# One scan over two channel groups instead of two scans in a selective-state-space kernel

## The chip, the cores and the metric

The program runs on 1 core of one Trainium2 chip, in one launch. The metric is the device time in microseconds (us). Before the change it was 1109.41 us, the median of three runs (1102.5 to 1112.57). The engines are named TensorE (PE in the rows, its weight loads PEld), VectorE (DVE), ScalarE (ACT), GpSimd (POOL) and SyncE (SP, which only issues transfers).

## The reference, cut to what matters

```python
xn = layernorm(x)                                    # (2, 1024, 512)
proj = xn @ W_in.T; x, gate = split(proj)            # 1024 channels each
x = silu(causal_conv4(x)); ssm = x @ W_x.T           # step sizes, B, C (16 states)
dt = softplus(rms(ts) @ W_dt.T + b_dt); A = -exp(A_log)
# scan over the 1024 tokens of a row, for each channel d and state n
state = state * exp(dt_t * A) + (dt_t * u_t) * B_t
y_t   = sum_n state * C_t
y = (y + x * D) * silu(gate);  s = y @ W_out.T
g = silu(top-2-of-8 mixture of experts(xn));         out = x + s * g
```

All is float32. The recurrence has 2 batch rows x 1024 channels x 16 states, 1024 tokens long. The rest (projections, the mixture of experts with its gather of rows, the output) is woven between the pieces of the recurrence.

## The kernel before, in words

**Tiling.** The 2048 tokens are cut into four chunks of `TC` = 512. Chunks 0 and 2 start a batch row ("even"), chunks 1 and 3 continue it ("odd"). A chunk has 8 tiles of 128 channels, so there are 32 tiles, numbered n. A tile has 128 x 16 recurrences; they are laid out over the 128 partitions in 16 units of 128 recurrences x 512 tokens. Four units are a quad (number m, four to a tile, 128 in all): its decays lie in the four banks of `sc` in PSUM (one bank holds 512 float32), its drives in one of four slots of `drive` in SBUF. Half a quad, two units side by side, is called a **pair** here: the low one (h = 0) and the high one (h = 1). There are 256 pairs.

**What a pair goes through.** GpSimd writes `drive` = dt*u*B for a quad (`drives`, L541), two quads or more ahead. ScalarE writes exp(dt*A) for the two units of a pair into `sc` (`decays`, L762), one ACTIVATE a unit. VectorE runs one scan a unit (`scans`, L1133) and multiplies both units by C (`products`, L1143). For 76 of the 128 low pairs GpSimd does that product instead (`low_products`, L554), and the scans of those write `drive`. TensorE sums the units of a channel (`sums`, L1391).

**What orders it.** Each engine has one queue, written out by hand tile by tile, and semaphores between the queues. `sc` has one copy: ScalarE may write the decays of a pair of quad m only when VectorE is done with the same pair of quad m - 1 (`low_ok`, `high_ok`, or `scan_ok` where GpSimd has the product). In even chunks ScalarE first copies the last column of both units to `state` (`keep_states`, L741) and waits for that copy; in odd chunks nothing is kept, and each scan starts from a column of `state`. ScalarE takes the pairs in the same order as VectorE, and between them its queue holds the softplus (L707 to L716), copies for the experts (L774, L785) and for the output (L798), the scaling of gathered rows (L831), and once a tile a block that no decay can pass: a table load, the silu of the gate, a table load (L906, L822, L914), just ahead of the decays of the high pair of the tile's third quad. That spot is called the **table place** here. In a unit's first scan VectorE waits only for the decay of that unit.

Of the kernel before, what the change touches and what calls it, by code (L numbers as in the profile page):

```python
# [7 lines left out]
ALU = mybir.AluOpType  # L8
ACT = mybir.ActivationFunctionType
# [8 lines left out]
PER_ROW = SEQ // TC  # L18
NT = D_IN // P
# [3 lines left out]
NQ = N // NG  # L23
CH = P // NG
NR = P // CH
# [7 lines left out]
RING = 4  # L33
# [39 lines left out]
def on_pool(m):  # L73
    return m % NQ in POOL_QUADS.get(m // NQ, ())


def dve_pairs(m):
    return m - pool_pairs(m)


def kept_states(m):
    c, rest = divmod(m, NQ * NT)
    kept = 2 * NQ * NT * ((c + 1) // 2)
    return kept + (2 * rest if c % PER_ROW < PER_ROW - 1 else 0)


def scan_moe(nc, x, wx_in, wg_in, wdt_in, wxp, wring, gate_w, means, a_log, conv_w, conv_b, d_skip,
             token_ids, route_consts, bc_dram, rep_rows, xn_rows, xnT_rows, order, slot_rows, s_rows, out):
    with ExitStack() as ctx:
        def sb(name, *shape, dtype=F32):  # L90
            return ctx.enter_context(nc.sbuf_tensor(name, [P, *shape], dtype))

        def ps(name, *shape):
            return ctx.enter_context(nc.psum_tensor(name, [P, *shape], F32))

        def sem(name):
            return ctx.enter_context(nc.semaphore(name))
# [3 lines left out]
        drive = sb("drive", RING, NR, TC)  # L101
        rep = sb("rep", 2, NR, 2, TC)
# [11 lines left out]
        x_pad = sb("x_pad", TC + K - 1)  # L114
        halo = sb("halo", NT, K - 1)
        no_halo = sb("no_halo", K - 1)
        t_e, t_w, t_l, t_r = sb("t_e", TC), sb("t_w", TC), sb("t_l", TC), sb("t_r", TC)
        dtu = sb("dtu", 2, TC)
        dt, u = dtu[:, 0, :], dtu[:, 1, :]
# [5 lines left out]
        state = sb("state", NT * UNITS)  # L125
        a_neg = sb("a_neg", NT * UNITS)
# [38 lines left out]
        sc = ps("sc_ps", NR, TC)  # L165
# [5 lines left out]
        first, second = x_ps[:, P:2 * P], x_ps[:, 2 * P:3 * P]  # L171
# [81 lines left out]
        abs_ok, exp_ok, ln_ok = sem("abs_ok"), sem("exp_ok"), sem("ln_ok")  # L253
        relu_ok, w_ok, log_mm = sem("relu_ok"), sem("w_ok"), sem("log_mm")
        sp_ok, dt_ok, dt_cp = sem("sp_ok"), sem("dt_ok"), sem("dt_cp")
        decay_ok, drive_ok, scan_ok = sem("decay_ok"), sem("drive_ok"), sem("scan_ok")
        state_ok = sem("state_ok")
        low_ok, high_ok, pool_ok = sem("low_ok"), sem("high_ok"), sem("pool_ok")
        sum_ok = sem("sum_ok")
        gated = sem("gated")  # L260
# [10 lines left out]
        def column(t, q, r):  # L271
            return t * UNITS + q * NR + r
# [7 lines left out]
        def drives_done(eng, count):  # L280
            eng.wait_ge(drive_ok, count)
# [193 lines left out]
        def _(pool):  # L475
# [68 lines left out]
            def low_products(m):  # L544
                n, q = divmod(m, NQ)
                if not on_pool(m):
                    return
                c, t = divmod(n, NT)
                pool.wait_ge(scan_ok, NR * m + 2)
                if c % PER_ROW < PER_ROW - 1:  # L550
                    pool.wait_ge(state_ok, kept_states(m) + 1)
                if t == 0:
                    pool.wait_ge(s_c[q], 16 * (c + 1))
                pool.tensor_tensor(drive[:, m % RING, 0:2, :], drive[:, m % RING, 0:2, :],  # L554
                                   c_all[:, q:q + 1, :].broadcast_to([P, 2, TC]), ALU.mult).then_inc(pool_ok, 1)
# [86 lines left out]
        def _(act):  # L642
# [88 lines left out]
            def keep_states(m, h):  # L731
                n, q = divmod(m, NQ)
                c, t = divmod(n, NT)
                if c % PER_ROW == PER_ROW - 1:
                    return
                lo = column(t, q, 2 * h)
                if h == 0 and on_pool(m):
                    last = drive[:, m % RING, 0:2, TC - 1]
                else:
                    last = sc[:, 2 * h:2 * h + 2, TC - 1]  # L740
                act.activation(state[:, lo:lo + 2], last, ACT.Copy).then_inc(state_ok, 1)  # L741

            def decays(m, h):
                n, q = divmod(m, NQ)
                if n >= TILES:
                    return
                t = n % NT
                if m:
                    if h:
                        act.wait_ge(high_ok, m)  # L750
                    elif on_pool(m - 1):
                        act.wait_ge(scan_ok, NR * (m - 1) + 2)
                    else:
                        act.wait_ge(low_ok, dve_pairs(m))
                    keep_states(m - 1, h)
                    if (m - 1) // (NQ * NT) % PER_ROW < PER_ROW - 1:
                        act.wait_ge(state_ok, kept_states(m - 1) + h + 1)
                if q == 0:
                    act.wait_ge(s_rep[n % 2][h], REP // 2 * (n // 2 + 1))
                for r in (2 * h, 2 * h + 1):  # L760
                    lo = column(t, q, r)
                    act.activation(sc[:, r, :], rep[:, n % 2, r, 0, :], ACT.Exp,  # L762
                                   scale=a_neg[:, lo:lo + 1]).then_inc(decay_ok, 1)

            def copy_slot_T(b, j):
                if j is None:
# [97 lines left out]
            act.copy(logit_T[:, :], f_ps[:, :]).then_inc(lgT_ok, 1)  # L864
            act.wait_ge(a_ok, 1)
            decays(0, 0)
            decays(0, 1)
            act.wait_ge(lg_d, 1)
            act.activation(weight, weight, ACT.Exp).then_inc(lg_e, 1)

            for n in range(TILES):
                c, t = divmod(n, NT)
                m = NQ * n
# [6 lines left out]
                if n:  # L880
                    decays(m, 1)
# [60 lines left out]
        def _(dve):  # L942
# [178 lines left out]
            def scans(m, h):  # L1121
                n, q = divmod(m, NQ)
                c, t = divmod(n, NT)
                if h == 0:
                    drives_done(dve, m + 1)
                follows = c % PER_ROW > 0
                if follows:
                    dve.wait_ge(state_ok, kept_states(m - NQ * NT) + h + 1)
                for r in (2 * h, 2 * h + 1):
                    lo = column(t, q, r)  # L1130
                    to = drive[:, m % RING, r, :] if h == 0 and on_pool(m) else sc[:, r, :]
                    dve.wait_ge(decay_ok, NR * m + r + 1)
                    dve.tensor_tensor_scan(to, sc[:, r, :], drive[:, m % RING, r, :],  # L1133
                                           state[:, lo:lo + 1] if follows else 0.0,
                                           ALU.mult, ALU.add).then_inc(scan_ok, 1)

            def products(m, h):
                n, q = divmod(m, NQ)
# [8 lines left out]
            def low(m):  # L1147
                scans(m, 0)
                if not on_pool(m):
                    products(m, 0)  # L1150

            def high(m):
                scans(m, 1)
                products(m, 1)
# [43 lines left out]
            for h in range(2):  # L1198
                scans(0, h)
                products(0, h)  # L1200
            route_weights()
            for n in range(TILES):
                c, t = divmod(n, NT)
                m = NQ * n
# [377 lines left out]
```

## Time and profile before

| | |
|---|---|
| median of three runs | 1109.41 us |
| profiled execution, own time | 1104.65 us |
| its span, first to last instruction | 1102.8 us |
| VectorE busy | 1025.4 us (93%) |
| GpSimd busy | 903.0 us (82%) |
| TensorE busy | 868.6 us (79%) |
| ScalarE busy | 730.2 us (66%) |

The profiled execution is one execution; what lies around its span is 1.85 us. The busy share is of the whole span; the first 84 us hold no scan of the recurrence. A row of the timeline with x2 is two instructions back to back, and its duration runs from the start of the first to the end of the second.

### The profile page before, as it was taken

What the parts mean: (1) busy time and instruction counts of PE and PEld (TensorE: products, weight loads), DVE (VectorE), ACT (ScalarE), POOL (GpSimd) and SP (SyncE); (2) the same over time, 40 slices, a digit from 0 to 9 for tenths busy, and PEclk for the clock granted to TensorE, in tenths of its full rate; (3) what the DMA queues carried; (4) which work ended last, traced back from release to release, by engine and by line L of the source; (5) the groups of instructions that cost most, each with busy time, mean ns of one, the idle gap of its engine ahead of it and who ended that gap; (6) DMA issues with size and microseconds to landing.
All of it is one profiled execution on the core that took longest, in us unless ns stands there. A gap on an engine that the chain in (4) does not pass through costs nothing.

```text
span 1102.8 us, 10141 instructions
## 1 busy us (share of the span) xinstructions
PE 868.6 (79%) x2722; PEld 317.1 (29%) x2722; DVE 1025.4 (93%) x1052; ACT 730.2 (66%) x1284; POOL 903.0 (82%) x353
## 2 busy tenths in 40 slices
PE   6954386899969998888854768989788998778577
PEld 3330122333323332333211222323223333223122
DVE  6759998999999999999999989999999989999997
ACT  2664666778766766777665766878767666666565
POOL 0019998998879899989889969798978978998895
PEclk9986678999989999999966979999998999799789
DMA  9345376656576566676743453865547656565714
GB/s 328 116 158 198 105 221 216 223 200 234 185 256 252 194 223 230 174 194 180 236 162 126 144 191 126 313 235 191 198 170 263 214 196 234 208 220 181 269 37 152
DMA packets 78089, 219.26 MB, mean 199 GB/s; under 512 B 15824, under 2 KB 17232, under 8 KB 71376
## 3 DMA queue, kind: packets, MB, share of 16 engines
q1 hardware_dynamic: 58096, 166.67, 44.4%
q10 hardware_dynamic: 12672, 31.46, 7.4%
q0 software_dynamic: 7264, 20.47, 6.7%
q8 instruction: 23, 0.38, 0.1%
q14 instruction: 34, 0.28, 0.1%
HBM read 176.85 MB, written 41.72 MB: 198 GB/s over the span
## 4 chain that ended last, share of the span: by engine, by line
DVE 34%; PE 24%; POOL 16%; issue 11%; ACT 7%; DMA 7%; SPq 1%; DVEq 0%; ACTq 0%; POOLq 0%
DVE sc_ps L1133 17%; POOL drive L541 10%; PE x_ps L1423 5%; DVE drive L1133 5%; PE f_ps L1376 4%; DVE drive L1143 3%; PE x_ps L1286 3%; POOL drive L554 3%; DMA rep<-rep_rows 3%; PE dt_ps L1351 3%; DMA x_slot<-xn_rows,slot_tok 3%; PE y_ps L1391 2%; DVE x_ps L1074 2%; PE sc_ps L1286 2%; ACT sc_ps L762 1%
## 5 line engine op out<-in xcount | busy, mean ns | idle before, releaser
L541 POOL TENSOR_TENSOR drive<-rep,b_all 128x2048 f32<-128x2048 f32 x128 | 580.3, 4538 | 118.1 <-DVEq L1017 77.4
L762 ACT ACTIVATE sc_ps<-rep,a_neg 128x512 f32<-128x512 f32 x512 | 332.0, 681 | 89.4 <-DVE drive L1143 63.1
L1133 DVE TENSOR_TENSOR_SCAN sc_ps<-sc_ps,state,drive 128x512 f32<-128x512 f32 x180 | 220.8, 1273 | 6.9 <-ACT sc_ps L762 6.9
L1143 DVE TENSOR_TENSOR drive<-sc_ps,c_all 128x1024 f32<-128x1024 f32 x180 | 220.4, 1224 | 6.2
L1391 PE MATMUL y_ps<-drive,stack 128*32 128x512 f32 x1024 | 156.7, 690 | 87.9 <-DVE drive L1143 60.4
L1133 DVE TENSOR_TENSOR_SCAN sc_ps<-sc_ps,drive 128x512 f32<-128x512 f32 x180 | 210.0, 1212 | 3.2 <-ACT sc_ps L762 2.3
L554 POOL TENSOR_TENSOR drive<-drive,c_all 128x1024 f32<-128x1024 f32 x76 | 179.3, 2359 | 23.3 <-ACT state L741 22.6
L1376 PE MATMUL f_ps<-w_ring,xT_slot 128*128 128x512 f32 x368 | 174.5, 619 | 14.4 <-ACT xT_slot L774 14.4
L1351 PE MATMUL dt_ps<-xnT,w_g 128*128 128x512 f32 x232 | 118.7, 659 | 21.3 <-ACT dtu L729 20.1
L1376 PEld LDWEIGHTS f_ps<-w_ring,xT_slot 128*128 128x128 f32 x368 | 70.5, 199 | 118.6 <-issue 118.3
L1133 DVE TENSOR_TENSOR_SCAN drive<-sc_ps,state,drive 128x512 f32<-128x512 f32 x76 | 93.1, 1266 | 2.8 <-ACT sc_ps L762 2.8
L1133 DVE TENSOR_TENSOR_SCAN drive<-sc_ps,drive 128x512 f32<-128x512 f32 x76 | 88.4, 1203 | 0.0
L1286 PE MATMUL x_ps<-xnT,w_x 128*128 128x512 f32 x192 | 88.2, 602 | 0.0
L1423 PE MATMUL x_ps<-w_out,xy 128*128 128x512 f32 x176 | 84.9, 629 | 0.0
L1391 PEld LDWEIGHTS y_ps<-drive,stack 128*32 128x32 f32 x1024 | 22.1, 114 | 185.5 <-issue 144.1
L1351 PEld LDWEIGHTS dt_ps<-xnT,w_g 128*128 128x128 f32 x232 | 46.5, 211 | 97.1 <-issue 97.1
L741 ACT ACTIVATE state<-sc_ps 128x2 f32<-128x2 f32 x90 | 15.1, 168 | 82.6 <-DVE drive L1143 80.5
L508 POOL DMA_INDIRECT x_slot<-xn_rows,slot_tok x46 | 45.5, 990 | 21.6 <-PE f_ps L1365 15.7
L1385 PE MATMUL y_ps<-xy,diag 128*128 128x512 f32 x64 | 37.5, 670 | 28.0 <-DVE xy L1160 28.0
L1365 PE MATMUL f_ps<-ident,x_slot 128*128 128x128 f32 x184 | 29.7, 286 | 33.3 <-DMA x_slot<-xn_rows,slot_tok 29.8
L1327 PE MATMUL dt_ps<-dt_in,w_dt 128*128 128x512 f32 x64 | 43.1, 762 | 15.2 <-DVE dt_in L1190 14.5
L1286 PEld LDWEIGHTS x_ps<-xnT,w_x 128*128 128x128 f32 x192 | 35.0, 190 | 52.4 <-issue 52.2
(184 smaller groups left out, 1057.7 us busy)
## 6 DMA issues: line engine op xcount, KB each, us to landing
rep<-rep_rows SPq DMA_DIRECT2D x128, 512.0 KB
w_ring<-wring SPq DMA_DIRECT2D x46, 1024.0 KB
rep_rows<-dtu ACTq DMA_DIRECT2D x32, 512.0 KB, 3.2
slot_rows<-y_slot ACTq DMA_DIRECT2D x46, 256.0 KB, 4.4
w_g<-wg_in SPq DMA_DIRECT2D x32, 256.0 KB
w_x<-wx_in SPq DMA_DIRECT2D x24, 256.0 KB
xn_rows<-rep SPq DMA_DIRECT2D x16, 256.0 KB, 2.5
b_all<-bc_rows SPq DMA_DIRECT2D x16, 256.0 KB, 4.4
```

Of the source, the lines that this page charges most:

```text
L508: pool.indirect_dma_start(x_slot[:, :], None, xn_rows[:, :], bass.IndirectOffsetOnAxis(ap=slot_tok[:, m:m + 1], axis=0)).then_inc(s_gx, 16)
L541: pool.tensor_tensor(drive[:, m % RING, :, :], rep[:, n % 2, :, 1, :], b_all[:, q:q + 1, :].broadcast_to([P, NR, TC]), ALU.mult).then_inc( ...
L554: pool.tensor_tensor(drive[:, m % RING, 0:2, :], drive[:, m % RING, 0:2, :], c_all[:, q:q + 1, :].broadcast_to([P, 2, TC]), ALU.mult).then ...
L762: act.activation(sc[:, r, :], rep[:, n % 2, r, 0, :], ACT.Exp, scale=a_neg[:, lo:lo + 1]).then_inc(decay_ok, 1)
L1133: dve.tensor_tensor_scan(to, sc[:, r, :], drive[:, m % RING, r, :], state[:, lo:lo + 1] if follows else 0.0, ALU.mult, ALU.add).then_inc(s ...
L1143: dve.tensor_tensor(drive[:, m % RING, 2 * h:2 * h + 2, :], sc[:, 2 * h:2 * h + 2, :], c_all[:, q:q + 1, :].broadcast_to([P, 2, TC]), ALU. ...
L1286: last = pe.matmul(x_bank(j), w(h), xnT[:, c % 2, h, :], start=(h == 0), stop=(h == HK - 1))
L1327: pe.matmul(dt_ps[:, :], w_dt[:, t, :], dt_in[:, :], start=True, stop=True).then_inc(dt_mm, 1)
L1351: mm = pe.matmul(gate_bank(c, t)[:, :], w_g[:, h, :], xnT[:, c % 2, h, :], start=(h == 0), stop=(h == HK - 1))
L1376: last = pe.matmul(f_ps[:, :], xT_slot[:, h, :], w_ring[:, j % 2, h, :], start=(h == 0), stop=(h == HK - 1))
L1391: last = pe.matmul(y_ps[CH * r:CH * (r + 1), :], stack[:, :], drive[:, m % RING, r, :], start=False, stop=(m % NQ == NQ - 1))
L1423: last = pe.matmul(bank, xy[:, c % 2, t, P * i:P * (i + 1)], w_out[:, t, :], start=(t == 0), stop=(t == NT - 1))
```

## The change

A pair's two scans become one over 1024 columns. Between the two units stands a decay of zero: ScalarE writes 0 to column 0 of the second unit's decays (a copy of one column from `no_halo`) and the exponentials to the other 511. With a decay of zero the second unit starts from its own first drive. In even chunks that is all. In odd chunks the second unit has a state to start from: ScalarE computes the exponential of the second unit's first column apart (`step1`) and, behind the two decays, adds `step1` * `state` to the first column of the second unit's drive, in place, after waiting for `step1_ok` and for GpSimd's drive. VectorE waits for the zero, for both decays and, in odd chunks, for that addition.

```diff
+def followers(m):
+    c, rest = divmod(m, NQ * NT)
+    return 2 * NQ * NT * (c // PER_ROW) + (2 * rest if c % PER_ROW else 0)
...
+        step1 = sb("step1", 2)
...
-                for r in (2 * h, 2 * h + 1):
-                    lo = column(t, q, r)
-                    act.activation(sc[:, r, :], rep[:, n % 2, r, 0, :], ACT.Exp,
-                                   scale=a_neg[:, lo:lo + 1]).then_inc(decay_ok, 1)
+                lo, odd = column(t, q, 2 * h), 2 * h + 1
+                act.activation(sc[:, odd, 0:1], no_halo[:, 0:1], ACT.Copy).then_inc(cut_ok, 1)
+                follows = n // NT % PER_ROW > 0
+                if follows:
+                    act.activation(step1[:, h:h + 1], rep[:, n % 2, odd, 0, 0:1], ACT.Exp,
+                                   scale=a_neg[:, lo + 1:lo + 2]).then_inc(step1_ok, 1)
+                act.activation(sc[:, 2 * h, :], rep[:, n % 2, 2 * h, 0, :], ACT.Exp,
+                               scale=a_neg[:, lo:lo + 1]).then_inc(decay_ok, 1)
+                act.activation(sc[:, odd, 1:], rep[:, n % 2, odd, 0, 1:], ACT.Exp,
+                               scale=a_neg[:, lo + 1:lo + 2]).then_inc(decay_ok, 1)
+                if follows:
+                    first = drive[:, m % RING, odd, 0:1]
+                    drives_done(act, m + 1)
+                    act.wait_ge(step1_ok, followers(m) + h + 1)
+                    act.activation(first, step1[:, h:h + 1], ACT.Identity, scale=state[:, lo + 1:lo + 2],
+                                   bias=first).then_inc(join_ok, 1)
...
-                for r in (2 * h, 2 * h + 1):
-                    lo = column(t, q, r)
-                    to = drive[:, m % RING, r, :] if h == 0 and on_pool(m) else sc[:, r, :]
-                    dve.wait_ge(decay_ok, NR * m + r + 1)
-                    dve.tensor_tensor_scan(to, sc[:, r, :], drive[:, m % RING, r, :],
-                                           state[:, lo:lo + 1] if follows else 0.0,
-                                           ALU.mult, ALU.add).then_inc(scan_ok, 1)
+                    dve.wait_ge(join_ok, followers(m) + h + 1)
+                lo, pair = column(t, q, 2 * h), slice(2 * h, 2 * h + 2)
+                to = drive[:, m % RING, pair, :] if h == 0 and on_pool(m) else sc[:, pair, :]
+                dve.wait_ge(cut_ok, 2 * m + h + 1)
+                dve.wait_ge(decay_ok, NR * m + 2 * h + 2)
+                dve.tensor_tensor_scan(to.rearrange("p r t -> p (r t)"), sc[:, pair, :].rearrange("p r t -> p (r t)"),
+                                       drive[:, m % RING, pair, :].rearrange("p r t -> p (r t)"),
+                                       state[:, lo:lo + 1] if follows else 0.0,
+                                       ALU.mult, ALU.add).then_inc(scan_ok, 2)
```

ScalarE's queue in tile 9 (an odd chunk), from the low pair ahead of the table place to the high pair behind it, before:

```order
L762 ACTIVATE sc_ps<-rep,a_neg 128x512 [waits scan_ok]
L762 ACTIVATE sc_ps<-rep,a_neg 128x512
L906 ACT_TABLE_LOAD
L822 ACTIVATE gate<-dt_ps 128x512 [waits gated,g_mm]
L914 ACT_TABLE_LOAD
L762 ACTIVATE sc_ps<-rep,a_neg 128x512 [waits high_ok]
L762 ACTIVATE sc_ps<-rep,a_neg 128x512
```

and the same place now:

```order
L769 ACTIVATE sc_ps<-no_halo 128x1 [waits scan_ok]
L772 ACTIVATE step<-rep,a_neg 128x1
L774 ACTIVATE sc_ps<-rep,a_neg 128x512
L776 ACTIVATE sc_ps<-rep,a_neg 128x511
L782 ACTIVATE drive<-step,drive,state 128x1 [waits step1_ok,drive_ok]
L926 ACT_TABLE_LOAD
L842 ACTIVATE gate<-dt_ps 128x512 [waits gated,g_mm]
L934 ACT_TABLE_LOAD
L769 ACTIVATE sc_ps<-no_halo 128x1 [waits high_ok]
L772 ACTIVATE step<-rep,a_neg 128x1
L774 ACTIVATE sc_ps<-rep,a_neg 128x512
L776 ACTIVATE sc_ps<-rep,a_neg 128x511
```

Three instructions of one column came to each pair, two ahead of its decays and one behind them.

VectorE's queue at the start of tile 8, the first of an odd chunk, before (the low pair, whose product GpSimd has; then the high pair):

```order
L1133 SCALAR_TENSOR_TENSOR drive<-sc_ps,state,drive 128x512 [waits decay_ok,state_ok,drive_ok]
L1133 SCALAR_TENSOR_TENSOR drive<-sc_ps,state,drive 128x512 [waits decay_ok]
L1110 TENSOR_TENSOR dtu<-dt_ps,xy 128x512 [waits s_dtu,x_ok,log_mm]
L1133 SCALAR_TENSOR_TENSOR sc_ps<-sc_ps,state,drive 128x512 [waits decay_ok,state_ok]
L1133 SCALAR_TENSOR_TENSOR sc_ps<-sc_ps,state,drive 128x512 [waits decay_ok]
```

and now:

```order
L1154 SCALAR_TENSOR_TENSOR drive<-sc_ps,state,drive 128x1024 [waits join_ok,cut_ok,state_ok,decay_ok,drive_ok]
L1130 TENSOR_TENSOR dtu<-dt_ps,xy 128x512 [waits s_dtu,x_ok,log_mm]
L1154 SCALAR_TENSOR_TENSOR sc_ps<-sc_ps,state,drive 128x1024 [waits cut_ok,join_ok,decay_ok,state_ok]
```

The two scans of a pair are one instruction, and it stands behind all that ScalarE does for the pair. Nothing else moves on this engine or on the others.

## Rows read from the trace of the kernel before

**Rows 1.** The page, part 1: busy us (share of span) x instructions.
```profile
PE 868.6 (79%) x2722; PEld 317.1 (29%) x2722; DVE 1025.4 (93%) x1052; ACT 730.2 (66%) x1284; POOL 903.0 (82%) x353
```

**Rows 2.** Windows, one a chunk: us; busy us (count) of each engine; clock; DMA.
```profile
84.60:336.10 251.50, 184.32 (x579) 64.22 (x578) 241.08 (x238) 173.53 (x329) 223.38 (x85) 0.86 0.60 203
336.10:594.60 258.50, 210.56 (x666) 74.86 (x664) 246.99 (x234) 175.56 (x288) 235.83 (x94) 0.92 0.61 194
594.60:847.70 253.10, 209.99 (x643) 76.33 (x644) 242.26 (x238) 180.65 (x340) 215.55 (x80) 0.93 0.58 204
847.70:1087.20 239.50, 194.09 (x616) 70.87 (x615) 227.16 (x204) 153.32 (x236) 215.95 (x85) 0.91 0.57 196
```

**Rows 3.** Groups by line, VectorE: busy us, mean ns | idle before, releaser.
```profile
L1133 DVE TENSOR_TENSOR_SCAN sc_ps<-sc_ps,state,drive 128x512 f32<-128x512 f32 x180 | 220.8, 1273 | 6.9 <-ACT sc_ps L762 6.9
L1143 DVE TENSOR_TENSOR drive<-sc_ps,c_all 128x1024 f32<-128x1024 f32 x180 | 220.4, 1224 | 6.2
L1133 DVE TENSOR_TENSOR_SCAN sc_ps<-sc_ps,drive 128x512 f32<-128x512 f32 x180 | 210.0, 1212 | 3.2 <-ACT sc_ps L762 2.3 <-POOL drive L541 0.8 <-DVE e_row L1050 0.2
L1110 DVE TENSOR_TENSOR dtu<-dt_ps,xy 128x512 f32<-128x512 f32 x32 | 21.9, 685 | 1.9 <-PE dt_ps L1338 1.1
L1016 DVE TENSOR_TENSOR_SCAN moe<-moe 128x128 f32<-128x128 f32 x1 | 0.4, 424 | 0.0
```

**Rows 4.** Timeline, VectorE: start us, us; an even pair, an odd one.
```profile
161.04 2.33 DVE L1133 TENSOR_TENSOR_SCAN drive<-sc_ps,drive 128x512 f32<-128x512 f32 x2
...
377.89 2.45 DVE L1133 TENSOR_TENSOR_SCAN drive<-sc_ps,state,drive 128x512 f32<-128x512 f32 x2
```

**Rows 5.** Groups by line, ScalarE.
```profile
L709 ACT ACTIVATE t_e<-t_e 128x512 f32<-128x512 f32 x32 | 20.2, 630 | 1.0
L815 ACT ACTIVATE diag<-ident,dsk 128x128 f32<-128x128 f32 x32 | 13.0, 407 | 0.0
L688 ACT ACTIVATE a_neg<-a_neg 128x128 f32<-128x128 f32 x1 | 0.3, 312 | 0.0
```

**Rows 6.** Timeline, ScalarE: two short instructions back to back.
```profile
28.67 0.19 ACT L676 ACTIVATE halo<-drive 128x3 f32<-128x3 f32 x1
28.76 0.20 ACT L692 ACTIVATE moe<-moe 128x12 f32<-128x12 f32 x1
```

**Rows 7.** Timeline at the table place of tile 9: ScalarE.
```profile
373.73 0.58 ACT L774 COPY xT_slot<-f_ps 128x512 f32<-128x512 f32 x1 [1.00 <-PE f_ps L1365]
374.39 1.30 ACT L762 ACTIVATE sc_ps<-rep,a_neg 128x512 f32<-128x512 f32 x2
375.71 1.28 ACT L906 ACT_TABLE_LOAD   x1
...
378.92 1.30 ACT L762 ACTIVATE sc_ps<-rep,a_neg 128x512 f32<-128x512 f32 x2
```

**Rows 8.** The same place: VectorE's next scan.
```profile
380.26 1.27 DVE L1133 TENSOR_TENSOR_SCAN sc_ps<-sc_ps,state,drive 128x512 f32<-128x512 f32 x1
```

**Rows 9.** Timeline, ScalarE: decays of the first and the last late pair.
```profile
162.62 1.30 ACT L762 ACTIVATE sc_ps<-rep,a_neg 128x512 f32<-128x512 f32 x2
...
1076.65 2.52 ACT L762 ACTIVATE sc_ps<-rep,a_neg 128x512 f32<-128x512 f32 x4
```

**Rows 10.** Timeline, VectorE: the scans of these two pairs.
```profile
163.35 2.35 DVE L1133 TENSOR_TENSOR_SCAN sc_ps<-sc_ps,drive 128x512 f32<-128x512 f32 x2
...
1077.45 2.46 DVE L1133 TENSOR_TENSOR_SCAN sc_ps<-sc_ps,state,drive 128x512 f32<-128x512 f32 x2 [2.48 <-ACT sc_ps L762]
```

**Rows 11.** Waits of VectorE: us in total, times, longest us.
```profile
DVE dt_ps L1114 <- ACT t_l L716: 18.7, 9, 4.5
DVE sc_ps L1133 <- ACT sc_ps L762: 9.1, 7, 2.5
DVE xy L1160 <- PE y_ps L1391: 4.3, 4, 1.3
DVE drive L1133 <- ACT sc_ps L762: 2.8, 3, 0.9
```

**Rows 12.** Timeline near a late drive: ScalarE, then GpSimd.
```profile
1052.66 1.28 ACT L762 ACTIVATE sc_ps<-rep,a_neg 128x512 f32<-128x512 f32 x2
1056.23 1.30 ACT L762 ACTIVATE sc_ps<-rep,a_neg 128x512 f32<-128x512 f32 x2 [2.29 <-DVE drive L1143]
...
1050.44 9.05 POOL L541 TENSOR_TENSOR drive<-rep,b_all 128x2048 f32<-128x2048 f32 x2
```

More of the change, by code:

```diff
@@ L255, in scan_moe @@
         sp_ok, dt_ok, dt_cp = sem("sp_ok"), sem("dt_ok"), sem("dt_cp")
+        cut_ok = sem("cut_ok")
         decay_ok, drive_ok, scan_ok = sem("decay_ok"), sem("drive_ok"), sem("scan_ok")
         state_ok = sem("state_ok")
+        step1_ok, join_ok = sem("step1_ok"), sem("join_ok")
         low_ok, high_ok, pool_ok = sem("low_ok"), sem("high_ok"), sem("pool_ok")
```

## The prediction

> **What bounds the kernel now.** I read the page's busy times first: VectorE is busy 1025.4 of 1102.8 us, GpSimd 903.0, ScalarE 730.2 [rows 1]. The windows by chunk say that this is no average over different stages: in each of the four, VectorE works 94 to 96% of the time (241.1 of 251.5, 247.0 of 258.5, 242.3 of 253.1, 227.2 of 239.5), while ScalarE is idle for 72 to 86 us and GpSimd for 23 to 38 us [rows 2]. So VectorE's time is the kernel's time, as long as its inputs are there, and time added to ScalarE costs only where VectorE comes to a pair whose decays are barely ready. The waits view shows that such places exist: VectorE waited ten times, 11.9 us, for decays, and nine times, 18.7 us, for the softplus [rows 11]. The question is how many pairs are close to that.
>
> For this I went through the timeline of both engines and took for each of the 256 pairs the **slack**: the start of its first scan less the end of its second decay. At tile 9's table place the second decay ends at 378.92 + 1.30 = 380.22 and the scan starts at 380.26 [rows 7, 8]: slack 0.04. Half of all pairs have more than 1.8 us. In 17 pairs it is negative, -0.36 to -0.58, since a first scan needs the first decay alone: the first is in tile 2 (decays 162.62 to 163.92, scan 163.35), the last in tile 31 (four decays from 1076.65 at 0.62 apart, the second ends near 1077.95, scan 1077.45) [rows 9, 10]. Four more have 0.04. These 21 are the short ones: 6 in even chunks, 15 in odd ones; 17 of them stand at a table place (12 of the 16 table places of odd chunks).
>
> **The gain on VectorE.** A lone scan of 512 columns takes 1212 ns without and 1273 ns with a state to read, one of 128 columns 424 ns [rows 3]. So a column is (1212 - 424) / 384 = 2.05 ns and 512 more are 1.051 us. The merged scan is then 1.212 + 1.051 = 2.26 us in even chunks and 1.273 + 1.051 = 2.32 us in odd ones (one state read instead of two), against 2.33 and 2.45 us for two [rows 4]: 0.067 and 0.126 saved, times 128 each, **-25 us**. The gain is small because the second scan starts before the first has ended (2 x 1.212 is 2.42, not 2.33). That a scan crosses from one PSUM bank into the next should cost nothing: the product over 1024 columns crosses it too and takes 1224 ns where 512 columns take 685, which is 1.05 ns a column. The 128-column scan reads SBUF; the cautious end takes for 512 more columns what the second scan adds now, 2.33 - 1.21 = 1.12 us: even pairs gain 0, odd ones 0.06, 7 us in all. I take 25, since both scans are paced by the same two steps a column.
>
> The rows show a fixed part of a scan of 424 - 128 x 2.05 = 161 ns, of which the overlap hides more than half. The Trainium skill (VectorE: DVE Perf Modes, on the TRN2 errata) says that the fixed cost lies between instructions, so that one large tile pays it once and several small ones each time, and (same page, on the DRAIN) that the next operation doesn't start until the pipe is empty. By that the whole fixed part would be saved; the x2 rows speak against it here, and its result is a rival below.
>
> **The cost on ScalarE.** An instruction of three columns takes 0.19 us, and the next starts 0.09 after it [rows 6]. A per-partition operand adds 0.095: 407 against 312 ns at 128 columns [rows 5]. So in ScalarE's queue the zero takes 0.09, `step1` (one operand) 0.18, the addition (two) 0.28; VectorE sees the end of the addition 0.33 after the second decay's. That is 0.09 for an even pair and 0.55 for an odd one, 128 x 0.64 = 82 us more on ScalarE. Most of it lies in ScalarE's own idle time (150 us in the even chunks, 169 in the odd ones [rows 2]). On the path is what falls on short pairs, with what ScalarE has added since its last idle time:
> - 15 odd short pairs. At a table place the pair ahead is done in the same breath (373.73 is the last start after idle time [rows 7]), so 0.55 + 0.27 + 0.33 = 1.15 is added before the scan, and where the slack is negative the scan also waits for the second decay, 0.5 more: six such of 1.67, two of 1.16 (idle time in front of them), four with slack 0.04 of 1.2: 17.1. Three others stand behind the copies of output tiles, at 1.13: 3.4. Two pairs with slack under 1 come in with 0.7 together.
> - 6 even short pairs: 0.09 to 0.18 added and 0.62 for the second decay, 0.8 each: 4.7.
>
> Sum **+26 us**, of which 9 are the wait for the second decay alone (ends: 9, if the short instructions cost nothing; 39, if none of them overlaps its neighbour, 0.19 + 0.285 + 0.38 an odd pair, by which 37 instead of 23 pairs come late).
>
> **Smaller terms.** The faster scans also shorten ScalarE's cover: between its last wait and the scan VectorE passes about two pairs, so at the short places their gain (12 x 0.25, 6 x 0.13) is given back: +4 us. Behind waits for another engine part of a delay is absorbed: the waits of `gate_tile` for TensorE (four, 4.3 us) and of the softplus, ahead of which ScalarE itself stood idle for TensorE's product: -4 us. The new wait of ScalarE for GpSimd's drive costs nothing: of the 64 low pairs in odd chunks only two have a drive that ends after the decays, and at the later one, 1054.97 against 1053.94, ScalarE stood idle until 1056.23 anyway [rows 12]. Queued behind it there are the next decays, which wait for VectorE. GpSimd has 23 us idle even in its fullest chunk [rows 2]; at 25 us less for the whole kernel it does not become the bound. TensorE waits for products and gets nothing new.
>
> **Sum**: -25 + 26 + 4 - 4 = +1 against the profiled execution's 1104.65, so 1105.7. That execution lies 4.8 below the median of the three runs, so in terms of the median **1110 us**. That is no change.
>
> **Rivals.**
> - *ScalarE's additions are hidden* (what ScalarE did before, it does no later): only the wait for the second decay remains, 9 us, and the absorption stays: -25 + 9 + 4 - 4 = -16, 1093 us. For it: ScalarE is idle a third of the time. Against: the 15 short odd pairs stand behind work that can't be passed. Chance 0.18, from 1093 to 1098.
> - *ScalarE becomes the bound of the odd chunks*, slower than before: if the short instructions don't overlap (the additions carry waits on two semaphores, and no row here shows so short a one), each odd pair holds the queue 0.86 and the late pairs cost 39: -25 + 39 + 4 - 4 = +14, **1124 us**. It decides from about 0.75 us an odd pair on. Chance 0.23.
> - *The whole fixed part is saved*: 161 ns an even pair and 161 + 61 an odd one, 49 us, less the 26: -23, 1087 us. It is the page's rule above; the overlapping x2 rows leave it 0.04.
> - *The long scan isn't cheaper*: a second bank costs something, or a column costs more in a longer run: gain 0 to 7, so +20 to +27, 1130 to 1136. For it: no scan over 1024 columns is in the trace. Against: the product's 1.05 ns. Chance 0.05.
> - The forecast, 1099 to 1120: 0.50.
>
> About 1% (11 us) is what a measurement of this kernel can tell from no change. Faster by more (under 1098): 0.18 + 0.04 = 0.22. Slower by more (over 1120.5): 0.23 + 0.05 less the part of the former that ends just below, and the upper tail of the forecast: 0.27. Same: 0.51. The range, with one in ten left out on each side, runs from 1095, inside the first rival, to 1131, between the second and the fourth. The likeliest case alone spans 1099 to 1120.
>
> **What would show it.** Right: scans of 1024 columns at 2.26 and 2.32 us; ScalarE 60 to 85 us busier or, with its overlaps, so much less idle; VectorE's waits for the zero, the decays or the addition at some 20 places, 12 of them at table places of odd chunks, 30 to 40 us in total where it was 11.9; VectorE's busy time near 1000 us. Wrong in the gain: a scan of 2.4 us. Wrong in the cost: an addition that starts more than 0.65 after its second decay's start, or waits spread over ordinary odd pairs. If VectorE's waits for decays stay under 20 us, the first rival has it.

## The result and the profile after

The change makes the kernel slightly slower: 1113.38 us (median of 20 runs) against 1106.78 (20 runs), a ratio of 1.0059 with a 95% interval of [1.0043, 1.0075], or 6.6 us. The profiled execution took 1115.1 us, 1113.3 of it its span; before the span was 1102.8.

The page's busy row after the change, which answers to [rows 1]:

```profile
PE 873.6 (78%) x2722; PEld 319.4 (29%) x2722; DVE 1004.2 (90%) x796; ACT 814.2 (73%) x1796; POOL 903.6 (81%) x353
```

VectorE works 21.2 us less (1025.4 before) and the span is 10.5 us longer, so VectorE is idle for 31.7 us more. ScalarE works 84 us more; the prediction had 82 in its queue. The groups by line show where both come from (busy us, mean ns | idle before, releaser); VectorE's answer to [rows 3]:

```profile
L1154 DVE TENSOR_TENSOR_SCAN sc_ps<-sc_ps,state,drive 128x1024 f32<-128x1024 f32 x90 | 211.3, 2347 | 25.6 <-ACT drive L782 17.5 <-ACT sc_ps L769 8.2
L1154 DVE TENSOR_TENSOR_SCAN sc_ps<-sc_ps,drive 128x1024 f32<-128x1024 f32 x90 | 205.8, 2286 | 11.5 <-ACT sc_ps L776 9.5 <-POOL drive L549 1.3 <-DVE e_row L1070 0.3
L1154 DVE TENSOR_TENSOR_SCAN drive<-sc_ps,state,drive 128x1024 f32<-128x1024 f32 x38 | 89.0, 2342 | 10.0 <-ACT sc_ps L769 9.2 <-ACT state L749 0.4 <-ACT drive L782 0.2
L1154 DVE TENSOR_TENSOR_SCAN drive<-sc_ps,drive 128x1024 f32<-128x1024 f32 x38 | 86.6, 2278 | 0.0
...
L782 ACT ACTIVATE drive<-step,drive,state 128x1 f32<-128x1 f32 x128 | 47.6, 372 | 0.0
L769 ACT ACTIVATE sc_ps<-no_halo 128x1 f32<-128x1 f32 x256 | 43.9, 171 | 63.8 <-DVE drive L1165 40.7 <-DVE drive L1154 7.6 <-issue 3.8
L772 ACT ACTIVATE step<-rep,a_neg 128x1 f32<-128x1 f32 x128 | 35.7, 279 | 0.0
```

A merged scan takes 2.28 us in even chunks and 2.35 in odd ones, where the prediction had 2.26 and 2.32 and two scans took 2.33 and 2.45. Before the scans VectorE now stands idle 47.1 us (25.6 + 11.5 + 10.0), where it was 12.9. The waits view says for whom (us in total, times, longest); it answers to [rows 11]:

```profile
DVE sc_ps L1154 <- ACT drive L782: 17.5, 13, 2.7
DVE dt_ps L1134 <- ACT t_l L724: 16.1, 6, 5.6
DVE sc_ps L1154 <- ACT sc_ps L776: 9.5, 6, 4.0
DVE drive L1154 <- ACT sc_ps L769: 9.2, 4, 2.3
...
DVE sc_ps L1154 <- ACT sc_ps L769: 8.2, 2, 4.5
```

L782 is the addition, L776 the second decay. Where L769 is named, the zero is the next pair's, which the scan does not need; the addition stands just ahead of it in ScalarE's queue, and that is what the scan waited for. The prediction expected 30 to 40 us of such waits, so 47.1 is beyond its sign of being right. Of the 34.2 us that were added, 28.7 stand before its 21 short pairs (summed over the timeline). The windows by chunk, which answer to [rows 2] (us; busy us and count of PE, PEld, DVE, ACT, POOL; clock; DMA):

```profile
85.60:339.10 253.50, 185.14 (x579) 64.43 (x578) 238.21 (x175) 179.76 (x395) 224.36 (x85) 0.86 0.60 201
339.10:603.00 263.90, 213.43 (x666) 76.06 (x664) 240.33 (x169) 210.90 (x478) 235.06 (x94) 0.90 0.57 189
603.00:855.10 252.10, 206.95 (x643) 75.37 (x644) 239.61 (x174) 187.02 (x406) 216.41 (x80) 0.95 0.59 206
855.10:1098.30 243.20, 196.69 (x613) 72.01 (x612) 220.76 (x139) 188.84 (x424) 216.31 (x86) 0.89 0.55 192
```

In these two executions the odd chunks, second and fourth, are 5.4 and 3.7 us longer; the even ones 2.0 longer and 1.0 shorter. In the odd ones ScalarE works 35 us more each.

The same table place as in [rows 7], tile 9, in ScalarE's timeline (start us, us):

```profile
377.72 0.17 ACT L769 ACTIVATE sc_ps<-no_halo 128x1 f32<-128x1 f32 x1 [0.21 <-DVE drive L1154]
377.83 0.28 ACT L772 ACTIVATE step<-rep,a_neg 128x1 f32<-128x1 f32 x1
378.01 0.67 ACT L774 ACTIVATE sc_ps<-rep,a_neg 128x512 f32<-128x512 f32 x1
378.63 0.67 ACT L776 ACTIVATE sc_ps<-rep,a_neg 128x511 f32<-128x511 f32 x1
379.24 0.37 ACT L782 ACTIVATE drive<-step,drive,state 128x1 f32<-128x1 f32 x1
379.63 1.28 ACT L926 ACT_TABLE_LOAD   x1
380.92 0.60 ACT L842 ACTIVATE gate<-dt_ps 128x512 f32<-128x512 f32 x1
381.54 1.28 ACT L934 ACT_TABLE_LOAD   x1
382.83 0.17 ACT L769 ACTIVATE sc_ps<-no_halo 128x1 f32<-128x1 f32 x1
382.94 0.28 ACT L772 ACTIVATE step<-rep,a_neg 128x1 f32<-128x1 f32 x1
383.12 0.67 ACT L774 ACTIVATE sc_ps<-rep,a_neg 128x512 f32<-128x512 f32 x1
383.74 0.67 ACT L776 ACTIVATE sc_ps<-rep,a_neg 128x511 f32<-128x511 f32 x1
384.35 0.37 ACT L782 ACTIVATE drive<-step,drive,state 128x1 f32<-128x1 f32 x1
```

and in VectorE's, where [rows 8] had no wait:

```profile
381.11 2.34 DVE L1154 TENSOR_TENSOR_SCAN drive<-sc_ps,state,drive 128x1024 f32<-128x1024 f32 x1
384.91 2.36 DVE L1154 TENSOR_TENSOR_SCAN sc_ps<-sc_ps,state,drive 128x1024 f32<-128x1024 f32 x1 [1.46 <-ACT drive L782]
```

ScalarE has no idle time from 377.72 to the addition that ends at 384.72, and VectorE stands still for 1.46 us in front of a pair that it used to reach 0.04 us after its second decay. The same 1.46 stands at eight of the 16 table places of the odd chunks. All table places together make 31.4 of the 47.1 us (7.9 of 12.9 before), summed over the timeline.

### The profile page after: what moved, and what is told of

The parts are those of the page before. It is cut to its first block, busy times and chain, and to the rows that moved or that the text cites. A ratio compares the mean times of both kernels' runs of the same rounds, so it can differ in the third digit from the quotient of the medians.

```text
span 1113.3 us, 10845 instructions
## 1 busy us (share of the span) xinstructions
PE 873.6 (78%) x2722; PEld 319.4 (29%) x2722; DVE 1004.2 (90%) x796; ACT 814.2 (73%) x1796; POOL 903.6 (81%) x353
## 4 chain that ended last, share of the span: by engine, by line
DVE 35%; PE 17%; POOL 15%; issue 12%; ACT 10%; DMA 8%; SPq 2%; DVEq 1%; ACTq 0%; POOLq 0%
DVE sc_ps L1154 18%; POOL drive L549 9%; DVE drive L1154 6%; PE x_ps L1445 5%; DMA rep<-rep_rows 4%; DVE drive L1165 3%; PE dt_ps L1373 3%; POOL drive L562 2%; DVE x_ps L1094 2%; PE y_ps L1413 2%; ACT sc_ps L776 2%; PE f_ps L1398 2%; DMA x_slot<-xn_rows,slot_tok 2%; DMA slot_rows<-y_slot 1%; ACT L934 1%
## 5 line engine op out<-in xcount | busy, mean ns | idle before, releaser
L1154 DVE TENSOR_TENSOR_SCAN sc_ps<-sc_ps,state,drive 128x1024 f32<-128x1024 f32 x90 | 211.3, 2347 | 25.6 <-ACT drive L782 17.5
L1154 DVE TENSOR_TENSOR_SCAN sc_ps<-sc_ps,drive 128x1024 f32<-128x1024 f32 x90 | 205.8, 2286 | 11.5 <-ACT sc_ps L776 9.5
L774 ACT ACTIVATE sc_ps<-rep,a_neg 128x512 f32<-128x512 f32 x256 | 172.2, 673 | 0.0
L776 ACT ACTIVATE sc_ps<-rep,a_neg 128x511 f32<-128x511 f32 x256 | 171.6, 670 | 0.0
L1373 PE MATMUL dt_ps<-xnT,w_g 128*128 128x512 f32 x232 | 125.3, 690 | 28.1 <-ACT dtu L737 28.1
L1154 DVE TENSOR_TENSOR_SCAN drive<-sc_ps,state,drive 128x1024 f32<-128x1024 f32 x38 | 89.0, 2342 | 10.0 <-ACT sc_ps L769 9.2
L769 ACT ACTIVATE sc_ps<-no_halo 128x1 f32<-128x1 f32 x256 | 43.9, 171 | 63.8 <-DVE drive L1165 40.7
L1154 DVE TENSOR_TENSOR_SCAN drive<-sc_ps,drive 128x1024 f32<-128x1024 f32 x38 | 86.6, 2278 | 0.0
```

The lines of the kernel that those rows point to most:

```text
L774: act.activation(sc[:, 2 * h, :], rep[:, n % 2, 2 * h, 0, :], ACT.Exp, scale=a_neg[:, lo:lo + 1]).then_inc(decay_ok, 1)
L776: act.activation(sc[:, odd, 1:], rep[:, n % 2, odd, 0, 1:], ACT.Exp, scale=a_neg[:, lo + 1:lo + 2]).then_inc(decay_ok, 1)
L1154: dve.tensor_tensor_scan(to.rearrange("p r t -> p (r t)"), sc[:, pair, :].rearrange("p r t -> p (r t)"), drive[:, m % RING, pair, :].rearr ...
L1373: mm = pe.matmul(gate_bank(c, t)[:, :], w_g[:, h, :], xnT[:, c % 2, h, :], start=(h == 0), stop=(h == HK - 1))
```

## The experiments

Each ran in five rounds against the kernel before, which beside them had medians of 1109.93 us (experiments 1 to 4), 1107.84 (5 to 8) and 1107.74 (9 to 12). A gain or loss in us is the ratio, less one, times that median; the plain difference of the two medians lies up to 1.4 us from it. Square brackets hold the 95% interval of the ratio. "Waits" is VectorE's idle time before the scans of the recurrence, summed over the timeline of one profiled execution; it was 12.9 us before and 47.1 after the change. Kernels that merge only some pairs do so by a function, and count their semaphores accordingly:

```diff
+def merged(m, h):
+    c, t, q = m // (NQ * NT), m // NQ % NT, m % NQ
+    return c % PER_ROW == 0
```

Here c is the chunk, t the tile of the chunk, q the quad of the tile, h the pair. Only the last line differs between these kernels.

**1. Even chunks alone**, by the line just shown.

> The merge in even chunks alone (no step1, no addition); odd chunks as before. Theory S (short places: VectorE gains by every merged scan and loses where ScalarE's decays are barely ready): gain 128 x 0.047 = 6 us, loss 5 to 6 us at the five or six short even pairs, so the time of before within 3 us. Rival P (another chain than VectorE's sets the pace, so the gain is worth nothing, and what the change costs is something else): 3 to 6 us over before.

Measured: 1108.43 against 1109.93 us, ratio 0.9985 [0.9964, 1.0006]. Where nothing is added to a drive, gain and loss cancel within the interval, as theory S had it: in the profiled execution VectorE is busy 5.4 us less and waits 7.7 us more before scans (20.6).

**2. Odd chunks alone.**
```diff
+    return c % PER_ROW > 0
```


> The merge in odd chunks alone, with step1 and the addition; even chunks as before. Theory S: the whole of the change's loss is here, gain 128 x 0.108 = 14 us, loss 20 to 22 us, so 5 to 9 us over before. If the loss comes from both kinds of chunk alike, 3 us.

Measured: 1117.64 us, ratio 1.0061 [1.0025, 1.0096], which is 6.8 us, as much as the whole loss. Waits 40.6 us.

**3. Without step1 and the addition.**
```diff
-                follows = n // NT % PER_ROW > 0
+                follows = False
...
-                    dve.wait_ge(join_ok, followers(m) + h + 1)
```


> All pairs merged, zero written, but without step1 and the addition (so the second unit of a pair in odd chunks starts from nothing: that part of the computation is left out). Theory S: gain 20 us kept, loss 9 us for the second decay and 3 for the zeros, so 5 to 10 us under before and 12 to 17 under the change. Rival P: the time of the change less at most 3 us. Rival D (the loss is the wait for the second decay, ScalarE's additions are hidden): within 3 us of the change.

Measured: 1106.16 us, ratio 0.9967 [0.9944, 0.9989], 3.7 us under before and so some 10 under the change; waits 31.5 us. The addition and step1 make the difference between a small gain and a small loss, which neither rival had. The gain is less than I expected.

**4. The wait for both decays alone.** Two scans, no zeros, nothing added:
```diff
-                    dve.wait_ge(decay_ok, NR * m + r + 1)
+                    dve.wait_ge(decay_ok, NR * m + 2 * h + 2)
```


> The kernel before, two scans, but the first scan of a pair waits for both decays. Theory S: 17 pairs with negative slack wait some 0.5 us longer, up to 9 us over before, 5 to 9 with what is absorbed. Rival D: 20 us or more over before (the whole loss, without the gain). Rival P: under 3 us.

Measured: 1111.47 us, ratio 1.0026 [1.0001, 1.005], 2.9 us; waits 24.3 us. A third of the 9 that the prediction gave to it, and less than the 5 to 9 of theory S. Rival D falls. Rival P, which had under 3 us, does not fall here: it takes experiments 5 and 10. The profiled execution took 1116.4 us, 4.9 above the median of its runs, and shows in part why the 9 was too much. Of the 17 pairs with negative slack seven wait 0.5 to 0.6 us longer than before, as predicted. The table places of tiles 10, 25 and 26 (slack -0.36) don't wait at all: in each of these tiles the low pair of the quad before, one of the seven, has waited the 0.6 us already. Of the 11.4 us of waits added in this execution 5.1 stand before three pairs, in tiles 3, 13 and 15, and why is open.

**5. All costs, no gain.** ScalarE does what it does in the change, into spare columns; VectorE waits for all of it and runs two scans:
```diff
-                act.activation(sc[:, odd, 0:1], no_halo[:, 0:1], ACT.Copy).then_inc(cut_ok, 1)
+                act.activation(spare1[:, h:h + 1], no_halo[:, 0:1], ACT.Copy).then_inc(cut_ok, 1)
...
-                    act.activation(first, step1[:, h:h + 1], ACT.Identity, scale=state[:, lo + 1:lo + 2],
+                    act.activation(spare1[:, 2 + h:3 + h], step1[:, h:h + 1], ACT.Identity, scale=state[:, lo + 1:lo + 2],
...
+                for r in (2 * h, 2 * h + 1):
+                    lo = column(t, q, r)
+                    to = drive[:, m % RING, r, :] if h == 0 and on_pool(m) else sc[:, r, :]
+                    dve.tensor_tensor_scan(to, sc[:, r, :], drive[:, m % RING, r, :],
```


> All that the change puts on ScalarE (a zero, step1 and the addition, written to spare columns, with the same waits) and VectorE waits for all of it and for both decays, but the two scans of a pair stay. Theory S: the loss without the gain, so the change's time plus the 21 us that its scans saved, less what is absorbed: 18 to 28 us over before. Rival P (the scans' gain was worth nothing): the time of the change, 6 to 8 us over before.

Measured: 1119.36 against 1107.84 us, ratio 1.0109 [1.0089, 1.013]: 12.1 us. Less than S, more than P. Its page has VectorE nearly as busy as before (1025.4) and ScalarE as busy as after:

```profile
PE 872.3 (78%) x2722; PEld 318.3 (29%) x2722; DVE 1023.5 (92%) x1052; ACT 814.1 (73%) x1796; POOL 903.9 (81%) x353
```

and its waits for ScalarE's work on a pair (L783 is the addition, L770 the next pair's zero, L777 the second decay) are

```profile
DVE sc_ps L1156 <- ACT spare L783: 13.5, 11, 2.4
...
DVE sc_ps L1156 <- ACT sc_ps L777: 6.9, 7, 2.2
DVE drive L1156 <- ACT spare L770: 5.5, 3, 1.9
...
DVE sc_ps L1156 <- ACT spare L770: 4.7, 2, 3.1
```

with 33.1 us in all before scans. At tile 9's table place, ScalarE's second decay and VectorE's scan:

```profile
383.12 0.67 ACT L777 ACTIVATE sc_ps<-rep,a_neg 128x512 f32<-128x512 f32 x1
...
384.19 2.47 DVE L1156 TENSOR_TENSOR_SCAN sc_ps<-sc_ps,state,drive 128x512 f32<-128x512 f32 x2 [1.15 <-ACT spare L783]
```

So the costs alone bring 20 us of waits before scans. VectorE's idle time anywhere else is 57.5 us (1114.1 - 1023.5 - 33.1), where it was 64.5, so some 7 of the 20 are absorbed there; the 12.1 us of the rounds put it at 8. The change itself, with 19 us less work on VectorE than this kernel, waits 14 us more before its scans (47.1). By the ratios (1.0109 - 1.0059) it is 5.5 us faster than this kernel, give or take 3. The 7 and the 14 come from one execution of each kernel, and this one's is the fastest of its six, 3.5 us under their median, so they can be off by some microseconds; that the gain is worth far less than the 19 to 21 us that it takes off VectorE rests on the rounds.

**6. Two scans at the table places.**
```diff
+    return not (q == 2 and h == 1)
```


> The change, but the high pair of each tile's third quad (the pair behind the table loads) keeps its two scans and its two plain decays; 224 of 256 pairs merged. Theory S: the waits at the table places were 31.5 us against 7.9 before; of the difference the zero, step1 and the end of the addition (0.6 us) and the wait for the second decay (0.5) go at 12 odd places, the 0.55 of the pair ahead of the loads stays; 2.6 us of gain are given up: 3 us under before to 2 over. Rival U (the loss is spread over all odd pairs, which queue one behind another): the time of the change within 2 us.

Measured: 1101.47 us, ratio 0.9951 [0.9934, 0.9969], 5.4 us under before, more than I expected; waits 24.1 us, 12.2 at table places. Undoing an eighth of the change turns its loss into a gain. Rival U falls.

**7. Two scans wherever the slack is short.**
```diff
+    return q != 2 and not (q == 1 and h == 0) if c % PER_ROW else not (q == 2 and h == 1)
```


> Merged only where the slack is long: in even chunks all but the pair behind the table loads, in odd chunks neither both pairs of the third quad nor the low pair of the second (the one behind the copies of output tiles); 112 + 80 pairs. Theory S: gain 112 x 0.047 + 80 x 0.108 = 14 us, loss 2 to 5, so 8 to 12 us under before. Rival U: 80 of the 128 odd pairs still carry three short instructions, so 5/8 of the loss and of the gain: 2 to 4 us over before.

Measured: 1102.09 us, ratio 0.9937 [0.9913, 0.9961]: 7.0 us under before, short of the 8 to 12, far from rival U. The 64 pairs left with two scans hold 20 of the 21 short ones. The table place of tile 9 in its trace, ScalarE and then VectorE, is that of the kernel before again, and without a wait:

```profile
378.76 1.28 ACT L940 ACT_TABLE_LOAD   x1
380.06 0.60 ACT L856 ACTIVATE gate<-dt_ps 128x512 f32<-128x512 f32 x1
380.67 1.28 ACT L948 ACT_TABLE_LOAD   x1
381.97 1.30 ACT L779 ACTIVATE sc_ps<-rep,a_neg 128x512 f32<-128x512 f32 x2
...
382.81 2.44 DVE L1168 TENSOR_TENSOR_SCAN sc_ps<-sc_ps,state,drive 128x512 f32<-128x512 f32 x2
```

**8. The reverse of 7**, merged only where 7 isn't:
```diff
+    return (q == 2 or (q == 1 and h == 0)) if c % PER_ROW else (q == 2 and h == 1)
```


> The reverse of the selective one: merged only in the 16 + 48 pairs that it leaves out. Theory S: gain 16 x 0.047 + 48 x 0.108 = 6 us, nearly the whole loss, so 8 to 16 us over before, more than the change itself, with a quarter of its merged scans. Rival U: 2 to 4 us over before.

Measured: 1114.91 us, ratio 1.0076 [1.0051, 1.0102]: 8.4 us over before with 64 merged pairs, where all 256 cost 6.6. The two intervals overlap, so whether a quarter of the edit costs more than the whole isn't shown; that it holds all of the loss is.

**9 and 10. Without the table loads**, in the kernel before and in the change alike. Both loads of a tile and one behind the loop go, and the silus from the main loop on are copies:
```diff
-                act.preload_act_table_set(SILU)
...
-                act.preload_act_table_set(LNEXP)
...
-                act.activation(gate[:, :], gate_bank(c, t)[:, :], ACT.Silu).then_inc(g_ok, 1)
+                act.activation(gate[:, :], gate_bank(c, t)[:, :], ACT.Identity).then_inc(g_ok, 1)
```


> The kernel before without the two table loads of each tile (the silus of the main loop are plain copies, so the silu of the gates, of three chunks' x and of the experts' output are left out). It removes 2.6 us of the block at each table place. Theory S: its own short places lose some 8 us of waits, little else: 4 to 12 us under before. It is the base for the next kernel.

> The change, with the same loads and silus left out. Theory S (the loss comes where the block of the table loads leaves no slack): with the block 2.6 us shorter the additions fit, and the gain shows: 4 to 14 us under the kernel before without the loads. Rival U (the loss is ScalarE's added work wherever it is): 5 to 8 us over it, as with the loads.

Measured: 1105.9 us for the kernel before without loads, ratio 0.9983 [0.9962, 1.0003] to the one with them, and 1098.7 us for the change without loads, ratio 0.9918 [0.9894, 0.9942]. The first is less than I expected: waits fell from 12.9 to 6.3 us, but VectorE's idle time elsewhere is 75.2 us (1107.7 - 1026.2 - 6.3), where it was 64.5. Between the two the change now **gains** 7.2 us (1098.7 / 1105.9 = 0.9935; its slowest run, 1100.94, is faster than the other's fastest, 1101.78), where with the loads it costs 6.6. The page of the change without loads:

```profile
PE 869.1 (79%) x2722; PEld 316.5 (29%) x2722; DVE 1006.1 (92%) x796; ACT 729.2 (66%) x1731; POOL 903.4 (82%) x353
```

and tile 9 in it, ScalarE and then VectorE: the additions are all there, but ScalarE has idle time at the place, and the scan does not wait. The waits of 1.46 us are gone at all eight places. Not all waits are: 22.2 us are left before scans, among them 2.3 us before each of the three short pairs behind the copies of output tiles, as in the change with loads.

```profile
376.87 0.58 ACT L842 ACTIVATE gate<-dt_ps 128x512 f32<-128x512 f32 x1
378.58 0.17 ACT L769 ACTIVATE sc_ps<-no_halo 128x1 f32<-128x1 f32 x1 [1.13 <-DVE drive L1162]
...
380.72 2.33 DVE L1151 TENSOR_TENSOR_SCAN sc_ps<-sc_ps,state,drive 128x1024 f32<-128x1024 f32 x1
```

**11 and 12. More pairs merged than in 7, and fewer instructions for it.** Experiment 11 merges 206 pairs:
```diff
+    return not ((q == 2 and (h == 1 or c % PER_ROW)) or (c % PER_ROW and t == 2 and q == 1 and h == 0))
```
and 12 computes step1 for the four quads of a tile at once, two instructions a tile:
```diff
+                if q == 0 and n // NT % PER_ROW > 0:
+                    firsts = a_neg[:, t * UNITS:(t + 1) * UNITS].rearrange("p (q r) -> p q r", r=NR)
+                    act.activation(step1[:, n % 2, h, :], firsts[:, :, 2 * h + 1], ACT.Exp,
+                                   scale=rep[:, n % 2, 2 * h + 1, 0, 0:1]).then_inc(step1_ok, 1)
```


> As the selective one, but more pairs merged: in even chunks all but the pair behind the table loads; in odd chunks all but the third quad's, and the second quad's low pair in the tiles 10 and 26 alone; 112 + 94 pairs. Theory S: 1.5 us more of gain than the selective one, one short pair (tile 25) more: 6 to 9 us under before.

> The same with step1 of all quads of a tile computed by two instructions at the tile's start instead of one a merged pair, which takes 0.18 us from each odd merged pair. Theory S: within 3 us of the wider one, since little of ScalarE's added work is on the path any more. Rival U: 4 to 6 us faster than it.

Measured: 1101.96 us, ratio 0.9948 [0.9924, 0.9971], and 1100.59 us, ratio 0.9938 [0.9916, 0.9961], against 1107.74. They are 5.8 and 6.9 us under before, the first just short of the 6 to 9 expected. The shared step1 gives 1.4 us by the medians, inside both intervals. Versions 6, 7, 11 and 12 beat both kernels and can't be told from each other.

## Why the prediction was right, and where its sizes were off

The forecast was no change, 1110 us in 1095 to 1131; measured was 1113.38, 0.6% over before. In the same 20 runs the kernel before had a median of 1106.78, not 1109.41, so the +1 of the sum (or the 0.6 over the median) stands against 6.6. The mechanism was right: a small gain on VectorE against waits at a few short places. That the sum came so near was luck in part, since the costs and the worth of the gain were both put too large and the errors cancelled.

- **What bounds the kernel, and the short places: shown.** The loss sits in the odd chunks (1, 2), at the places with little slack (6, 7, 8), and turns to a gain when ScalarE's block there is shortened (9, 10). Of the 21 pairs that the prediction counted as short, all were waited for after the change. (Summed again over the timeline, half of all pairs have more than 2.2 us of slack, not 1.8. Nothing hangs on it.)
- **The gain: 25 us predicted, 19.6 us measured.** A pair takes 0.047 us less in even chunks and 0.106 in odd ones, 128 times each; the whole engine is busy 21.2 us less. The long scan's second 512 columns cost 2.10 ns each (2286 - 1212 over 512), not 2.05: either the 128-column scan, the only row for the slope, was slightly off, or the second bank costs up to 0.02 us a scan, which no run tells apart. The Trainium skill (VectorE: DVE Perf Modes, TRN2 errata) says that one large tile pays the fixed cost once and several small ones each time. The trace agrees in part: merging saved 19.6 us, where the whole fixed part, the third rival, would have been 49, since two scans in a row overlap.
- **The cost at the short places: +26 predicted, 20 us of waits in experiment 5**, which has the costs alone. The sizes of the short instructions were right: the zero holds the queue 0.11 us, step1 0.18, the addition 0.28 (0.39 before a table load, which starts only when it has ended), predicted 0.09, 0.18, 0.28. At the table places of tiles 8, 9, 24 and 27, with slack 0.04, the wait is 1.15 us, predicted 1.2. The term that was too large is the wait for the second decay, 9 us in the sum: alone it cost 2.9. At the eight odd table places with negative slack the prediction had 1.67 us six times and 1.16 twice; at four of them (tiles 10, 25, 26 and 28) it is 1.15, the same as with slack 0.04. The half microsecond was added to each pair as if it stood alone, but in tiles 10, 25 and 26 a wait at one pair gave a later one its slack back (4).
- **The smaller terms were mis-sized too.** Absorbed were not 4 us but 7 to 8. In experiment 5's trace they are in the very waits that the prediction named: the softplus (18.7 to 15.5 us) and TensorE's `y_ps` (4.3 to 1.3). And given back were not 4 us of the gain but about 14: 19.6 us of gain make 5.5 us of time, give or take 3, so the part given back is 11 to 17. At eight table places the two traces show what happened. The wait is 1.15 us without the gain and 1.46 with it. Of the 0.31 between, 0.22 is what VectorE's two scans of pairs between ScalarE's last wait and this scan save, as the prediction had counted. The other 0.09 is no gain given back: the merged scan starts 0.50 us after the end of the second decay (384.91 - 384.41), the two scans 0.40 after it (384.19 - 383.79), and no run says why. These eight places make only 2.5 of the 14 us. Some 6 more stand before four pairs, in tiles 2, 13, 15 and 31, whose waits also differ between kernels without additions: before the pair behind tile 15's loads 1.7 us in the kernel before, 4.4 in experiment 4, 3.1 in experiment 5, 4.5 in the change. So the size of this term is shown by the rounds; where most of it went is open.
- **Taken together**, the gain was worth 5.5 us and the costs 12.1, where the prediction had 25 - 4 = 21 and 26 - 4 = 22. The gain's worth was put almost four times too large and the costs nearly twice, and their difference was near all the same.
- **The rivals.** Hidden additions: no, the kernel without them is 10 us faster than the change (3). ScalarE as the bound of the odd chunks: no, since it has 53 and 54 us idle in them (263.9 - 210.9, 243.2 - 188.8); it bounds single places. The whole fixed part saved, or nothing: no, 19.6 us lie between their 49 and their 0 to 7. (The last one's sum comes to +19 to +26, not +20 to +27.) The two semaphores of the addition cost nothing: it starts 0.61 us after the second decay's start, as a decay does.

What stays open besides: why removing the loads gave the kernel before 2 us and not the 6.6 by which its waits before scans are shorter. Its trace shows 10.7 us more idle time elsewhere, but its profiled execution is 3.7 us above its median. The profiled executions of one kernel differ by some microseconds, and there is one of each, so pieces of this size can't be read from them.

## What to carry to other kernels

Before work is moved from the busiest engine to an idle one, measure the slack at each handover, not the idle share: here ScalarE was idle a third of the time, and 64 of 256 handovers still held the whole loss. A speed-up of the busy engine can be waited away at the next place that another engine times: here 19.6 us of gain made 5.5 us of time. The same edit, applied everywhere but at those places, went from 0.6% slower to 0.6% faster.

## What the runs showed of the hardware

In a scan over 1024 columns across two PSUM banks the second 512 columns cost 2.10 ns each; between 128 and 512 columns it was 2.05. Two scans back to back overlap: two of 1.21 us take 2.33, two of 1.27 take 2.45. So merging them saved 0.05 us in even chunks and 0.11 where the second had a state to read, not the fixed part of a scan, which is 0.16 and 0.22 by the prediction's slope and 0.14 and 0.20 by the measured one. The three instructions of one column on ScalarE took 0.17 us (the zero, no per-partition operand), 0.28 (step1, one) and 0.37 (the addition, two), but the next one started 0.11, 0.18 and 0.28 after their start; they also differ in function and target, so the operands are only one reading of the steps. A table load started only when the addition ahead of it had ended, 0.39 us after its start.
